# QKV, attention, second routing and experts as one block of engine programs

## The reference

```python
x = x + 0.5 * ffn(ln(x), W_gate, b_gate, W_e, b_e)
x = x + attn(ln(x), Wqkv, q_ln_w, q_ln_b, k_ln_w, k_ln_b, Wout)
x = x + 0.5 * ffn(ln(x), W_gate, b_gate, W_e, b_e)

def ffn(x, ...):          # 8 experts, 512 x 512 each, the best 2 of each token
    top_idx = top_k(x @ W_gate + b_gate, 2)
    return mean over the two of relu(x @ W_e[e] + b_e[e])

def attn(x, ...):         # 32 heads of 16, causal, ALiBi
    q, k, v = split(clip(x @ Wqkv.T, -8, 8));  q, k = layer_norm(q), layer_norm(k)
    probs = softmax(q @ k.T / 4 + slope * (j - i), causal)
    return (probs @ v) @ Wout.T
```

## Time and profile before

| what | us |
|---|---|
| three runs | 1029.15 median, 1027.4 to 1030.22 |
| the profiled execution | 1029.65 |
| its span | 1027.9 |
| what lies around the span | 1.75 |
| routing 1 ends, experts 1 ends (first instruction of the next block) | about 90, 244.6 |
| QKV ends, attention ends | about 437, 746 |
| routing 2 ends | about 874 |

### The profile page before, as it was taken

How to read it: one execution, slowest core, us unless ns; L and a number is a source line. 1 busy time by engine, 2 the same in 40 slices (tenths; PEclk the granted TensorE clock), 3 DMA queues, 4 the chain that set the end, 5 groups by cost and what they waited for, 6 DMA issues and landing times. The chain is left out here.

```text
span 1027.9 us, 19987 instructions
## 1 busy us (share of the span) xinstructions
PE 858.6 (84%) x6562; PEld 606.2 (59%) x6563; DVE 647.3 (63%) x1290; ACT 449.6 (44%) x834; POOL 350.1 (34%) x338
## 2 busy tenths in 40 slices
PE   3656999981999987689999999999768972899993
PEld 1245888861777766555555555555355642788872
DVE  7965444434989867567777777777248877344431
ACT  3531333322254543527777777777533330233330
POOL 7722777752122222200000000000054421577763
PEclk9886999995999999959999999999979995899997
DMA  9982678762264698656665556662178951578863
GB/s 344 368 298 75 122 147 146 138 112 62 65 197 154 175 221 219 198 135 136 147 135 133 133 144 134 134 134 74 33 246 283 309 192 45 114 147 145 152 112 47
DMA packets 112602, 162.06 MB, mean 158 GB/s; under 512 B 16608, under 2 KB 74080, under 8 KB 112256
## 3 DMA queue, kind: packets, MB, share of 16 engines
q1 hardware_dynamic: 94672, 123.84, 42.0%
q0 software_dynamic: 17856, 37.25, 19.4%
HBM read 97.43 MB, written 67.37 MB: 160 GB/s over the span
## 5 line engine op out<-in xcount | busy, mean ns | idle before, releaser
L829 DVE TENSOR_REDUCE att_part<-att_s_ps 128x2 f32<-128x1024 f32 (+2 forms) x160 | 195.5, 1225 | 63.5 <-PE att_s_ps L677 63.0
L791 ACT ACTIVATE att_prob<-att_st_ps 128x512 f32<-128x512 f32 x320 | 173.7, 595 | 80.2 <-PE att_st_ps L703 80.2
L144 PE MATMUL exp_z_ps<-ex_w_hi,exp_xT_hi 128*128 x312 | 131.9, 423 | 1.7 <-issue 0.8
L146 PE MATMUL exp_z_ps<-ex_w_hi,exp_xT_lo 128*128 x312 | 125.8, 403 | 0.0
L145 PE MATMUL exp_z_ps<-ex_w_lo,exp_xT_hi 128*128 x312 | 125.4, 402 | 0.0
L1500 ACT ACTIVATE exp_y<-exp_y 128x512 f32<-128x512 f32 x72 | 45.5, 632 | 169.6 <-DVE exp_y L1519 169.6
L1507 DVE TENSOR_TENSOR exp_xT_lo<-exp_t_ps,exp_xT_hi 128x512 fp32r<-128x512 f32 x78 | 53.9, 691 | 103.9 <-ACT exp_xT_hi L1493 103.9
L1128 POOL TENSOR_TENSOR ex_w_lo<-ex_w_lo,ex_w_hi 128x1024 fp32r<-128x1024 f32 x32 | 76.3, 2396 | 90.0 <-ACT ex_w_hi L1253 59.4
L716 PE MATMUL att_pv_ps<-att_prob,att_v_sb 128*32 128x256 f32 (+2 forms) x1280 | 101.4, 391 | 1.8 <-ACT att_oT L796 1.8
L641 POOL CAST att_m_parts<-att_part 128x28 fp32r<-128x28 f32 x32 | 6.6, 206 | 272.4 <-DVE att_part L833 272.4
L1519 DVE TENSOR_TENSOR exp_y<-exp_z_ps,ex_bias 128x512 f32<-128x512 f32 x72 | 49.8, 691 | 67.9 <-PE exp_z_ps L146 67.9
(11 more groups left out here) (211 smaller groups left out, 1662.3 us busy)
## 6 DMA issues: line engine op xcount, KB each, us to landing
ex_w_lo<-in_L_ffn_W_e SPq DMA_DIRECT2D x32, 512.0 KB, 7.2
v_vals<-st_vals SPq DMA_DIRECT2D x16, 512.0 KB, 2.9
q_parts<-st_partq SPq DMA_DIRECT2D x32, 256.0 KB, 3.4
k_parts<-st_partk SPq DMA_DIRECT2D x32, 256.0 KB, 3.9
att_v_sb<-v_vals SPq DMA_DIRECT2D x32, 256.0 KB, 3.6
ex_bias<-in_L_attn_hidden_states SPq DMA_DIRECT2D x8, 512.0 KB, 7.6
acc<-ex_bias SPq DMA_DIRECT2D x8, 512.0 KB, 8.7
xn<-ex_rows SPq DMA_DIRECT2D x8, 512.0 KB, 5.6
```

The lines of the kernel that those rows point to most:

```text
L144: nc.tensor.matmul(out, x_hi[:, s], w_hi(c), start=(c == 0), stop=False)
L146: last = nc.tensor.matmul(out, x_lo[:, s], w_hi(c), start=False, stop=(c == C - 1))
L791: nc.scalar.activation(prob[n % 2][:, col:col + 512], st_ps[(e + half) % 3][:, :], ACT.Exp).then_inc(exp_done, 1)
L829: nc.vector.tensor_reduce(out, src, X_AXIS, ALU.max, negate=True).then_inc(red_done, 1)
```

## The change

There are two blocks in place of six: routing 1 with experts 1, and all the rest in one. Both are opened with `no_gpsimd_drain=True` (the engines but POOL drain, and the barrier is one of semaphores alone), and the barrier after the clearing too is of semaphores alone. `route_block` returns its engine programs in parts, which attention calls at set places; what the barriers kept apart is now kept apart by semaphores that the stages share (`Freed`, `st.unit_done` and so on) and by where tiles lie in SBUF and PSUM.

```diff
     nc.clear_and_free_semaphores(Memory.sems)
-    nc.all_engine_barrier()
+    nc.all_engine_barrier(sem_only=True)
...
# attention, SP: in iteration 20, and after the loop
+                if n == NG - 3 * AHEAD:
+                    route.sync_begin(sp)
+            route.sync_next(sp)
             store(NG - 1)
...
# attention, POOL: ahead of its loop, and behind it
+            route.gpsimd_begin(pool)
...
+            route.gpsimd_split(pool)
...
# attention, PE
+            for s in range(2):
+                pe.wait_ge(st.clip_done[s], TILES)
+            pe.wait_ge(st.lo_done, TILES)
+            scores(0, 0)
+            scores(0, 1)
+            last_turns()
+            for u in range(2, S_UNITS):
                 scores(0, u)
...
+                if n == NG - 2:
+                    route.tensor_begin(pe)
             for piece in range(5):
                 values(NG - 1, piece)
+            route.tensor_first(pe)
             turn_out(NG - 2)
             turn_out(NG - 1)
...
# attention, ACT: after the copies of Wout, and in iteration 31 ahead of its exponentials
+            route.scalar_split(act)
...
+                if n == NG - 1:
+                    route.scalar_begin(act)
...
# attention, DVE: in iteration 31, behind combine(31)
+                if n == NG - 1:
+                    route.vector_begin(dve)
...
# routing
-        lg_ps = route_ps if proj else wq_ps[3]
+    lg_ps = t_ps[0] if proj else wq_ps[3]
-        root = m.sb("root", [P, 4])[:, :] if proj else route_ps[:, 0:4]
+    root = route_ps[:, 0:4]
+    EARLY = 6 if proj else 2
...
+    def sync_begin(sp):
+        if proj:
+            load_o(0)
+            load_o(1)
+        load_x(0)
+        sp.dma_start(g_raw...)
+        sp.dma_start(bg...)
+        load_x(1)
+        for n in range(EARLY):
+            load_weights(n)
+
+    def sync_next(sp):
+        load_o(2)
+        load_o(3)
+        load_weights(EARLY)
+        load_weights(EARLY + 1)
...
+    def transpose(t):
+        pe.wait_ge(xn_done, t + 1)
+        at_least(pe, copied, t - 1)
+        if proj and t % 2 == 0:
+            at_least(pe, lg_out, t // 2)
...
+    def tensor_begin(pe):
+        pe.wait_ge(ident_done, 1)
+        pe.wait_ge(freed.red_done, S_UNITS * NG)
+        o_transpose(0)
+        o_transpose(1)
+
+    def tensor_first(pe):
+        pe.wait_ge(wo_lo_done, 1)
+        pe.wait_ge(freed.m_rows_done, NG)
+        out_proj(0)
+        o_transpose(2)
+
+    def scalar_split(act):
+        nc.scalar.activation(wo_hi, wo_turned, ACT.Copy).then_inc(wo_hi_done, 1)
+    def scalar_begin(act):
+        o_split(0)
+        o_split(1)
+    def vector_begin(dve):
+        o_rest(0)
+        o_rest(1)
+    def gpsimd_split(pool):
+        pool.wait_ge(wo_hi_done, 1)
+        nc.gpsimd.tensor_tensor(wo_lo, wo_turned, wo_hi, ALU.subtract)
...
# end of routing, POOL
-            ex.gather(nc, xn_dram, 0, ex.rows[:, 0, :])
+        for s in range(C):
+            ex.gather(nc, xn_dram, s, ex.rows[:, s, :])
...
# experts
+            for r in range(RING):
+                sp.wait_ge(added[r], 16 * ((N - 1 - r) // RING + 2))   # was POOL's
+            pool.wait_ge(ex.lists_done, 1)
-            for s in range(1, AHEAD):
+            for s in range(C, AHEAD):
                 gather(s)
```

More of the change, by code:

```diff
@@ L802, in _ @@
                                      ACT.Copy).then_inc(wo_out, 1)
+            for r in range(C):
+                act.wait_ge(wo_out, r + 1)
+            route.scalar_split(act)
             for n in range(NG):
@@ L1419, in expert_block, with turn_wq @@
-def expert_block(nc, prefix, ex, xn_dram, acc, spare=None):
+            if 1 <= u <= PAIRS:
+                transpose(2 * u - 2)
+                transpose(2 * u - 1)
+            if u >= 2:
+                turn_logits(u - 2)
+        def turn_wq(n):
+            pe.wait_ge(wq_loaded[n % 2], 16 * (n // 2 + 1))
+            for k in range(2):
+                at_least(pe, wq_out, 2 * n + k - 3)
+                transpose4(wq_ps[(2 * n + k) % 4], w_stage[n % 2][:, k, :]).then_inc(wq_tr, 1)
+        if w_qkv is not None:
+            turn_wq(0)
+            turn_wq(1)
@@ new lines, in tensor @@
+        last.then_inc(rank_done, 1)
+        if w_qkv is not None:
+            turn_wq(2)
+            turn_wq(3)
+        for n in range(2 * TILES):
+            pe.wait_ge(onehot_done, n + 1)
+            nc.tensor.matmul(id_ps, at_col[:, n % COL_RING, :], at_tile[:, n, :, :].rearrange("p a s -> p (a s)"),
+                             start=(n == 0), stop=(n == 2 * TILES - 1)).then_inc(ids_done, 1)
+        if w_qkv is not None:
+            turn_wq(4)
+            turn_wq(5)
+    def scalar_split(act):
+        nc.scalar.activation(wo_hi[:, :, :], wo_turned[:, :, :], ACT.Copy).then_inc(wo_hi_done, 1)
@@ new lines, in route_block, with o_split, copy, logits_out @@
+    act = nc.scalar
+    def o_split(t):
+        act.wait_ge(o_tr, t + 1)
+        at_least(act, y_done, t - 1)
+        nc.scalar.activation(oT_hi[t % 2][:, :], o_ps[t % 2][:, :], ACT.Copy).then_inc(o_hi, 1)
+    def copy(t):
+        act.wait_ge(tr_done, t + 1)
+        at_least(act, lg_done, t // 2)
+        nc.scalar.activation(xT[:, t % 2, :], t_ps[t % 2][:, :], ACT.Copy).then_inc(copied, 1)
+    def logits_out(u):
+        if u == 0:
+            act.wait_ge(bias_loaded, 16)
+        act.wait_ge(lg_done, u + 1)
+        at_least(act, gate_done, u)
+        nc.scalar.activation(lgT, lg_ps[0:E, 0:2 * P], ACT.Identity, bias=bg[:, 0:1]).then_inc(lg_out, 1)
@@ new lines, in weights, with scalar @@
+    def weights(n):
+        act.wait_ge(w_loaded[n % WR], 16 * (n // WR + 1))
+        nc.scalar.activation(ex.w_hi[:, 2 * n:2 * n + 2, :], ex.w_lo[:, 2 * n:2 * n + 2, :].bitcast(F32),
+                             ACT.Copy).then_inc(w_hi_done, 1)
+    def scalar_begin(act):
+        o_split(0)
+        o_split(1)
+    def scalar(act):
+        for u in range(PAIRS + 1):
+            if proj and u + 1 < PAIRS:
+                o_split(2 * u + 2)
+            if u < PAIRS:
+                weights(2 * u)
+            if proj and u + 1 < PAIRS:
+                o_split(2 * u + 3)
+            if u >= 2:
+                logits_out(u - 2)
+            if u >= 1:
+                copy(2 * u - 2)
+                copy(2 * u - 1)
+            if u < PAIRS:
+                weights(2 * u + 1)
+        logits_out(PAIRS - 1)
+        if w_qkv is not None:
+            for t in range(2 * WQ_PAIRS):
+                act.wait_ge(wq_tr, t + 1)
+                out, bank = w_turned[:, :, t * P:(t + 1) * P], wq_ps[t % 4][:, :].rearrange("p (c n) -> p c n", c=C)
+                if t < 2 * C:
+                    out = out.rearrange("p c (d h) -> p c d h", h=8)
+                    bank = bank.rearrange("p c (h d) -> p c d h", h=8)
+                nc.scalar.activation(out, bank, ACT.Copy).then_inc(wq_out, 1)
@@ L1554, in bias_rows @@
+        expert_block(nc, block, "exp2", ex, xn, acc2, side="right")
 def bias_rows():
```

956 lines of the change are left out of this document (466 added, 490 removed).

## The result

The changed kernel takes 1011.85 us (median of 4 runs, 1010.26 to 1013.01) beside 1029.36 us of the kernel before: a ratio of 0.983, with a 95% interval of 0.981 to 0.985. It is faster by 17.5 us. The prediction had said 1003, within 991 to 1013: the sign and that range hold, and the forecast gave the change 9 us too much. It lies outside the narrower range of the forecast itself (996 to 1009), in the band of 1009 to 1016 that was kept for the rival of the drain. That rival did not happen, as the experiments show, so that the wide range held by luck and not by its reason.

What follows compares the result with a forecast made beforehand. PE bounds attention; no engine bounds routing 2, a pipeline, so each seam was costed by itself. Terms sum to 26.4 us off 1029.65, giving 1003.2, said as 1003; own range 996 to 1009, wide range 991 to 1013.

Steps and rivals of the forecast that it cites:

- the rival of the drain: POOL's drain is paid elsewhere, giving back up to 12.7 us: 1009 to 1016 us; chance 0.18.
- two drains: End of both expert blocks: POOL's drains of 6.35 us go away, 12.7 us less; bounds 0 and 12.7.
- QKV to attention: Seam before attention: earlier scores, but later last turns and Wout load; net gain 2.4 us, bounds 0 and 8.
- twelve loads: Transfers put on SP in attention's iteration 20 delay the maxima of group 22: 8 us lost once, bounds 2.5 and 12.
- attention to routing 2: First out-projection's work moves into attention's last iterations; out-projection 1 starts at 746.8, not 760.12: gain 13.3 us, bounds 11 and 14.5.
- rounds of routing 2: Gains of 2.5 us in the first two rounds and 1.2 in the last, against 3.7 lost to a new wait.
- experts' starts: Both expert blocks: gathers 0 to 3 issued in one go, first product 3.0 us earlier each, 6.0 in all.
- The late issue: SP issues `max_rows(22)` in attention about 3.8 us late; from issue alone PE stands for 2.5 us.
- the new wait: Routing 2: `lg_ps` shares `t_ps[0]`, so `transpose(2u - 2)` waits for ACT's `logits_out(u - 2)`; 0.74 us in five rounds, 3.7 lost.
- The root in PSUM: Routing 2: removes DVE's 2.31 us stall at line 86; worth 0 in steady rounds, 1.2 us in the last.
- The signs that I had named: Expected in the trace: no POOL drains, QKV's first load about 235, one PE gap of some 6 us, 11.2 us rounds.
- The gap at the transposes of Wout: Start of attention: PE waits for Wout's load and transposes right after it lands; absence would prove the prediction wrong.

Runs made afterwards that it cites:

- start: Changed kernel with pieces spread over iterations 21 to 26, logits copied before the split, Wout loaded ahead of v, POOL's constants behind its first maxima: 989.88 us, ratio 0.962.
- ACT's order: Changed kernel, but in routing ACT copies the logits out before it splits tile 2u + 3, not behind that: 1001.18 us, ratio 0.973.
- the pieces spread: Changed kernel, but the six weight pieces are issued one per iteration, 21 to 26, not all in iteration 20: 1002.42 us, ratio 0.974.
- one gather: Changed kernel, but both routings end with the gather of tile 0 only; tiles 1 to 3 are gathered in the experts' part: 1016.38 us, ratio 0.986.
- all: As "start", plus QKV's last turns ahead of the second scores, and x, gate's weights and pieces spread over iterations 20 to 27: 985.35 us, ratio 0.956.
- the changed kernel again: The changed kernel, unaltered, measured a second time beside the last group of runs on one chip: 1011.36 us, ratio 0.980.

## Why the prediction was right, and where its size was off

| term | forecast | measured in the trace |
|---|---|---|
| two drains | 12.7 | 6.44 + 6.3 = 12.7 |
| QKV to attention | 2.4 | 3.5 |
| twelve loads | -8.0 | -14.0 |
| attention to routing 2 | 13.3 | 2.85 + 10.48 = 13.3 |
| rounds of routing 2 | 2.5 + 1.2 - 3.7 = 0 | -3.3 |
| experts' starts | 6.0 | 1.2 + 3.1 |

These add up to 16.5 of 16.6 us, as they must, since the points divide the whole span; how well a single term is known is another matter (above).

- **Drains, right.** Shown twice, and by themselves. The rival that something else pays for them is out.
- **Attention to routing 2, right to the tenth**, with `out_proj(0)` before the two `turn_out`, the 1.2 us of later values (4.15 - 2.85 = 1.3 measured), and out-projection 1 in place. The tenth is luck: in the second trace of the same kernel the last values run at half clock, and 1.7 us of it are gone.
- **QKV to attention, right in its first half.** The turns came 2.7 us later than the shift of QKV alone, as worked out (3.1). But Wout was issued at 432.25 and not where I put it: SP's last stores and the loads of v took less time to issue than I had put, and it landed in 6.7 us in place of 7.6; both are within what the traces scatter by. Against the trace of the kernel before, the nine traces with this seam gain between 1.5 and 3.8 us, and 2.0 less each against the other trace with the old seam, so that the forecast of 2.4 was as good as the 3.5 measured here. Then POOL's constants, which I had called hidden behind the wait for Wout, became a wait of their own of 3.48 us. In the run "start" 1.0 us of it was left.
- **The twelve loads: the step that failed in size.** The mechanism holds: one stall at `scores_by_key(22, 0)`, a slow stretch behind it, and no other. The late issue was 4.9 us (3.8 forecast) and would have cost 3.3 with the other loads (2.5 forecast as the lower bound). The bytes cost 8.3, where "about 6.5" for all left them 4.0. The failing sentence is "At that rate 4.5 MB take 13 to 14 us, and the loads of group 25 behind them 4.7": from the first of the loads to PE's start it gave 19 us, and the trace has 651.45 - 628.08 = 23.4. In that stretch 6.3 MB moved, at 271 GB/s, where the forecast had 5.75 MB at 325 for the large part. The 325 were too high in the kernel before already. I had worked them out from the 2 MB that I took to move in those 6.2 us, and the window of the trace over them has 289 (columns as above):

```profile
774.49:780.68 6.19, 4.57 (x21) 2.67 (x19) 5.67 (x20) 0.62 (x1) 2.38 (x1) 1.00 0.92 289
```

I also shaved the share of the group's own loads ("somewhat less when packed"). The slow stretch cost 2.4, not 1.5. The 14.0 lie 2 us outside my bound of 12.

- **The rounds: the new wait under-priced, and the clock left out.** From gate to gate the -3.3 are 1.6 gained by the first gate (2.5 forecast) and 1.6 in the last two rounds (1.2 forecast), 4.8 lost by the new wait (3.7 forecast), and 1.7 lost in one gate that was computed at half clock, of which the forecast had nothing. The wait at `transpose(2u - 2)` is there, 1.12 us, five times. The root in PSUM brought nothing to the steady rounds, as forecast; with ACT's order repaired it was worth 4 to 5.9 us at the ends of the routing, where the forecast saw the last round alone.
- **Starts: right in size (2.9 and 2.7 us from gather 0 to the first product), wrong in cause by half.** On the clock the first gave 1.2, since gather 0 came 0.6 later and the experts' 39 tiles took 1.05 more. Over the fourteen traces that stretch lasts 137.1 to 140.9 us, whatever the kernel, so I don't count it to the change.
- **The signs that I had named.** One wait for maxima, no drain under another line, no long step of the root and rounds of about 11.2 us (11.4) came as written. QKV's first load came at 236.98 and not 235. The gap at the transposes of Wout, whose absence was to prove me wrong, was all but absent here (0.33 us), since POOL's maxima had taken its place; the second trace of the same kernel has it (2.29).

Not tried: the same burst from another queue, and a sweep over how many pieces fit into one iteration.

## What to carry to other kernels

A load put into the slack of a queue is priced by what is latency-bound behind it, not by the queue's mean share: twelve loads cost 14 us in one iteration, and with the six large ones spread 0.8, 4.5 and 1.6 us in three traces. When two tiles share a bank to save room, look at once at the order on the engine that frees the bank; one line moved on ACT gave back 7 to 10 us, where the sharing had seemed to cost 5. And before a large rewrite of seams, switch off the drain alone: here that was most of the gain.

## What the runs showed that I had not expected

The clock falls within a phase that is not idle. In the changed kernel PE waited 1.12, then 0.52 us ahead of one gate, and was granted half clock from that gate's start on (columns as above):

```profile
775.46:777.40 1.94, 1.94 (x9) 0.75 (x10) 1.63 (x10) 0.89 (x1) 0.97 (x1) 1.00 1.08 414
784.00:786.86 2.86, 1.28 (x10) 1.05 (x11) 2.38 (x8) 2.05 (x5) 0.77 (x1) 1.00 0.96 380
786.86:788.70 1.84, 1.84 (x5) 0.65 (x6) 1.53 (x10) 0.89 (x1) 0.87 (x1) 0.51 1.03 414
788.70:790.40 1.70, 1.70 (x6) 0.31 (x3) 1.70 (x2) 0.00 (x0) 1.47 (x1) 0.53 0.50 202
790.40:793.00 2.60, 2.60 (x12) 2.14 (x12) 0.51 (x2) 0.00 (x0) 0.00 (x0) 1.00 0.52 184
```

In five of the rounds the waits are the same, and only one meets it; in other runs it is another gate (807.59 with the pieces spread, 772.44 and 833.88 with one gather, 811.80 in "all", 837.57 in the changed kernel again), each 1.3 to 1.7 us longer. Of the seven traces with those waits five have such a gate in routing 2, and of the five with ACT's order two. It needs no shared bank: in the kernel before with the drains alone taken out, the last gate is a long one too (838.47, 2.83 us). That the short waits make it likelier is possible, but so few traces don't show it.
